# Two 64-row mask matmuls in the row half of their scores, and the values of two heads in one group of 32 columns

## The reference

```python
x = x + attn_a(layernorm(x))   # 16 heads of 8 channels, causal
x = x + ffn(layernorm(x))      # 8 experts, top 2 of each token
x = x + attn_b(layernorm(x))   # 16 heads of 8 channels
x = x + ffn(layernorm(x))

# attn_a
scores = einsum('bhqd,bhkd->bhqk', q, k) / sqrt(8)
attn = softmax(scores + triu(NEG, k=1))
out = einsum('bhqk,bhkd->bhqd', attn, v).transpose(0, 2, 1, 3).reshape(b, t, d)
return out @ wo + bo
```

## Time and profile before

| what | us |
|---|---|
| time, median of 3 runs | 1162.33 |
| lowest, highest | 1160.31, 1164.01 |
| the profiled execution, its span | 1164.9 |
| PE busy | 1029.9 (88%) |
| DVE busy | 755.5 (65%) |
| ACT busy | 672.4 (58%) |
| POOL busy | 525.5 (45%) |
| weight loads of PE | 716.6 (62%) |

### The profile page before, as it was taken

How to read it: one execution, slowest core, us unless ns; L and a number is a source line. 1 busy time by engine, 2 the same in 40 slices (tenths; PEclk the granted TensorE clock), 3 DMA queues, 4 the chain that set the end, 5 groups by cost and what they waited for, 6 DMA issues and landing times.

```text
span 1164.9 us, 28879 instructions
## 1 busy us (share of the span) xinstructions
PE 1029.9 (88%) x9290; PEld 716.6 (62%) x9290; DVE 755.5 (65%) x2322; ACT 672.4 (58%) x1399; POOL 525.5 (45%) x980
## 2 busy tenths in 40 slices
PE   2998999897989999999798979999888799999990
PEld 1444555453468989999443434444443589999990
DVE  4687778877777333456777888888877663334442
ACT  2365676663644545556277858897757445455550
POOL 2243444332742610344687736455736436004455
PEclk9998999996989999999778979998888899999995
DMA  6446544562235878887544323343221469778873
GB/s 152 104 114 138 116 110 99 151 181 57 54 118 174 271 233 236 260 255 236 125 111 104 101 56 85 89 107 84 65 49 44 130 191 280 227 242 256 272 225 109
DMA packets 201723, 175.03 MB, mean 150 GB/s; under 512 B 19812, under 2 KB 160616, under 8 KB 201576
## 3 DMA queue, kind: packets, MB, share of 16 engines
q1 hardware_dynamic: 193384, 156.41, 49.1%
q0 software_dynamic: 8192, 16.79, 4.8%
HBM read 122.99 MB, written 50.14 MB: 149 GB/s over the span
## 4 chain that ended last, share of the span: by engine, by line
PE 60%; DVE 11%; issue 6%; POOL 5%; DMA 4%; SPq 3%; ACT 1%; POOLq 0%; ACTq 0%; DVEq 0%
PE psS L1358 9%; PE psT L1365 9%; PE psO L321 8%; PE psS L355 7%; PE psO L1381 4%; PE psN L1381 4%; DVE mx L671 4%; PE psS L386 3%; PE psT L363 3%; POOL xn L1259 3%; PE psM L276 2%; PE psN L328 2%; DMA eo<-ysb 2%; PE psN L337 1%; PE psM L1346 1%
## 5 line engine op out<-in xcount | busy, mean ns | idle before, releaser
L671 DVE TENSOR_REDUCE mx<-psS 128x3 f32<-128x384 f32 (+1 forms) x512 | 311.4, 617 | 119.5 <-PE psS L386 61.8
L355 PE MATMUL psS<-kst,qst 48*128 48x256 bf16 (+1 forms) x1024 | 201.7, 286 | 46.4 <-DVE mx L671 33.2
L558 ACT ACTIVATE pT<-psT,scb 128x512 f32<-128x512 f32 x256 | 193.9, 777 | 43.2 <-PE psT L363 40.7
L363 PE MATMUL psT<-qst,kst 50*128 50x256 bf16 (+1 forms) x1024 | 194.7, 278 | 4.6 <-DMA qst<-scr_m 2.2
L1422 DVE TENSOR_TENSOR hT<-sg,psT 128x512 f32<-128x512 f32 x142 | 97.5, 686 | 154.4 <-PE psT L1365 127.7
L1245 POOL DMA_INDIRECT xg<-xn,slot x128 | 123.1, 962 | 131.3 <-DVE ysb L1417 72.1
L1358 PE MATMUL psS<-xTt,wgc 128*128 128x128 f32 x1136 | 153.7, 279 | 5.7 <-issue 5.3
L355 PEld LDWEIGHTS psS<-kst,qst 48*128 48x128 bf16 x1024 | 66.2, 97 | 146.0 <-DVE mx L671 68.2
L1365 PE MATMUL psT<-xTt,wuc 128*128 128x128 f32 x1136 | 152.2, 278 | 1.5 <-DMA wuc<-in_L_ffn_Wu 1.4
L790 POOL TENSOR_SCALAR_AFFINE_SELECT pT<-pT 128x256 f32<-128x256 f32 x224 | 90.6, 412 | 133.0 <-ACT pT L553 131.8
L553 ACT ACTIVATE pT<-psT 128x384 f32<-128x384 f32 x256 | 122.9, 490 | 46.1 <-PE psT L363 35.9
(11 more groups left out here) (225 smaller groups left out, 1595.1 us busy)
## 6 DMA issues: line engine op xcount, KB each, us to landing
wgc<-in_L_ffn_Wg SPq DMA_DIRECT2D x142, 256.0 KB, 3.1
wuc<-in_L_ffn_Wu SPq DMA_DIRECT2D x142, 256.0 KB
scr_part<-part SPq DMA_DIRECT2D x128, 128.0 KB, 2.1
qst<-scr_part SPq DMA_DIRECT2D x64, 192.0 KB, 3.7
kst<-scr_part SPq DMA_DIRECT2D x64, 192.0 KB, 4.7
xin<-xg SPq DMA_DIRECT2D x142, 64.0 KB
eo<-ysb SPq DMA_DIRECT2D x142, 64.0 KB
scr_part<-part SPq DMA_DIRECT2D x32, 192.0 KB, 1.9
```

The source lines that it names most:

```text
L355: return nc.tensor.matmul(ps[:, c0:c0 + n], q_[r64, t, q0], k_[r64, t, 0:n], start=(half == 0), stop=True, skip_group_check=True)
L363: return nc.tensor.matmul(ps[:, c0:c0 + T - q0], k_[m64, t, half * P:half * P + P], q_[m64, t, q0:T], start=(half == 0 or not L.causal), s ...
L558: nc.scalar.activation(pT[:, g % 8, 0:cols], psT[g % 2][:, 0:cols], ACT.Exp, scale=scb[r][:, 0, i:i + 1], bias=scb[r][:, 1, i:i + 1]).then ...
L671: nc.vector.tensor_reduce(mx3[:, u, 0:n, pos:pos + 1].rearrange("p a b -> p (a b)"), psS[h % 2][:, 0:kcols(L)].rearrange("p (a k) -> p a k ...
```

## The change

The mask of a head becomes two matmuls of 64 rows each, which lie in the half of the rows that the scores of this head use. The triangles are built anew so that each half of the rows holds a 64-row piece of them; the weights are rows of the identity for the piece on their own half of the partitions, and rows of `identx`, the identity with its column halves exchanged, for the other. The first piece of `trib` covers 128 columns of each diagonal block, the second the last 64. The same is done with `tritb` for the last two batches.

Quads 0 and 2, and quads 1 and 3, now share a group of 32 partitions: the values start at column 16 of a head's 32, and the weights of quads 2 and 3 are read 16 columns further on, so that their values fall on columns 16 to 24 where those of quads 0 and 1 fall on 0 to 8; the four products add up in bank `psO[0]`. So `oT` has two pieces, not four: one copy by ACT at head 2, two transposes at heads 4 and 11. `normalise` picks the heads out of 16-column pieces.

```diff
+HALF_P = P // 2
...
+        identx = sb("identx", [P, P], BF16)
...
-        vp = [sb(f"vp{r}", [P, 2, H, 32]) for r in range(RING)]
+        vp = [sb(f"vp{r}", [P, 2, H * 32 + 16]) for r in range(RING)]
...
-        oT = sb("oT", [P, 4, T])
+        oT = sb("oT", [P, 2, T])
...
-                if q % 2 == 0:
-                    after(pe, s["oT"], 2 * (b - 1) + q // 2 + 1)
+                if q == 0:
+                    after(pe, s["oT"], b)
+                pair, region = q // 2, q % 2
...
-                        o0 = (q % 2) * T
-                        last = nc.tensor.matmul(psO[q // 2][32 * i:32 * i + 32, o0 + dst[0]:o0 + dst[1]],
-                                                vp[r][:, kb, h, :], pT[:, h % 8, src[0]:src[1]],
-                                                start=(kb == 0), stop=(kb == 1), skip_group_check=True)
+                        o0, v0 = region * T, 32 * h + 16 * (1 - pair)
+                        last = nc.tensor.matmul(psO[0][32 * i:32 * i + 32, o0 + dst[0]:o0 + dst[1]],
+                                                vp[r][:, kb, v0:v0 + 32], pT[:, h % 8, src[0]:src[1]],
+                                                start=(q == 0 and kb == 0), stop=(pair == 1 and kb == 1),
+                                                skip_group_check=True)
...
             def out_transposes(qb):
-                for q in range(4):
+                for q in range(2):
...
+            def mask_half(bank, group, half, tri, t0, c0, n):
+
+                rows = slice(HALF_P * group, HALF_P * group + HALF_P)
+                select = identb if half == group else identx
+                diag = bank[:, 0:3 * P].rearrange("p (a k) -> p a k", a=3)[:, 0:3:2, c0:c0 + n]
+                return nc.tensor.matmul(diag, select[rows, :],
+                                        tri[rows, t0:t0 + n].unsqueeze(1).to_broadcast([HALF_P, 2, n]),
+                                        start=False, stop=True, skip_group_check=True)
...
                     if L.causal and bT >= MASKED:
-                        diag = psT[1 - par][:, 0:3 * P].rearrange("p (a k) -> p a k", a=3)[:, 0:3:2, :]
-                        last_t = nc.tensor.matmul(diag, identb[:], tritb[:].unsqueeze(1).to_broadcast([P, 2, P]),
-                                                  start=False, stop=True, skip_group_check=True)
+                        last_t = mask_half(psT[1 - par], 1 - par, 0, tritb, HALF_P, 0, HALF_P)
+                        last_t = mask_half(psT[1 - par], 1 - par, 1, tritb, 0, 0, P)
                     last_t.then_inc(s["ST"], 1)
                 if S_ and L.causal:
-                    last_s = nc.tensor.matmul(psS[par][:, 0:3 * P].rearrange("p (a k) -> p a k", a=3)[:, 0:3:2, :],
-                                              identb[:], trib[:].unsqueeze(1).to_broadcast([P, 2, P]),
-                                              start=False, stop=True, skip_group_check=True)
+                    last_s = mask_half(psS[par], par, 0, trib, 0, 0, P)
+                    last_s = mask_half(psS[par], par, 1, trib, 0, HALF_P, HALF_P)
...
-            def evac_oT(b, half):
-                after(act, s["PV"], 4 * b + 2 * half + 2)
+            def evac_oT(b):
+                after(act, s["PV"], 4 * b + 4)
                 after(act, s["tO_ps"], 2 * b)
-                nc.scalar.activation(oT[:, 2 * half:2 * half + 2, :], psO[half][:].rearrange("p (a t) -> p a t", a=2),
+                nc.scalar.activation(oT[:], psO[0][:].rearrange("p (a t) -> p a t", a=2),
                                      ACT.Copy).then_inc(s["oT"], 1)
...
-                if h == 13 and T_:
-                    evac_oT(bT, 0)
...
-                o4 = psN[:].rearrange("p (h c) -> p h c", c=32)
-                nc.vector.reciprocal(rden[:], o4[:, :, HD]).then_inc(s["rden"], 1)
+                o4 = psN[:, 0:2 * P].rearrange("p (m a c) -> p m a c", a=2, c=2 * HD)
+                den = rden[:].rearrange("p (m a) -> p m a", a=2)
+                nc.vector.reciprocal(den, o4[:, :, :, HD]).then_inc(s["rden"], 1)
...
-            nc.gpsimd.affine_select(out=trib[:], in_=trib[:], compare_op=ALU.is_ge, fill=NEG, base=0,
-                                    pattern=[[-1, P]], channel_multiplier=1).then_inc(s_const, 1)
-            nc.gpsimd.affine_select(out=tritb[:], in_=tritb[:], compare_op=ALU.is_ge, fill=NEG, base=0,
-                                    pattern=[[1, P]], channel_multiplier=-1).then_inc(s_const, 1)
+            for group in range(2):
+                rows = slice(HALF_P * group, HALF_P * group + HALF_P)
+                pool.wait_ge(s_const, 4 + 2 * group)
+                nc.gpsimd.affine_select(out=trib[rows, :], in_=trib[rows, :], compare_op=ALU.is_ge, fill=NEG, base=0,
+                                        pattern=[[-1, P]], channel_multiplier=1).then_inc(s_const, 1)
...
             nc.vector.tensor_copy(identb[:], ident[:]).then_inc(s_const_dve, 1)
+            nc.vector.tensor_copy(identx[:, 0:HALF_P], ident[:, HALF_P:P]).then_inc(s_const_dve, 1)
+            nc.vector.tensor_copy(identx[:, HALF_P:P], ident[:, 0:HALF_P]).then_inc(s_const_dve, 1)
```

More of the change, by code:

```diff
@@ L243, in build, with heads_of @@
         LB.s["pT"] = LB.s["exp"]
+        def heads_of(v):
+            return v[:, :, 0:32 * H].rearrange("p k (h c) -> p k h c", c=32)
         def kcols(L):
@@ L251, in pe_setup @@
             pe.wait_ge(s["wp"], 4)
-            pe.wait_ge(s_const_dve, 2)
+            pe.wait_ge(s_const_dve, 4)
             for o in range(2):
@@ L433, in pe_step @@
                 if h == 4 and O_:
-                    after(pe, s["oT"], 2 * bO + 2)
+                    after(pe, s["oT"], bO + 1)
                     if T_:
@@ L534, in act_step @@
                 if h == 2 and O_:
-                    evac_oT(bO, 1)
+                    evac_oT(bO)
                 if h == (3 if L.causal else 4) and P_:
@@ L639, in normalise @@
                 after(dve, s["onT_ps"], 2 * bO + qb)
-                o4 = psN[:].rearrange("p (h c) -> p h c", c=32)
-                nc.vector.reciprocal(rden[:], o4[:, :, HD]).then_inc(s["rden"], 1)
+                o4 = psN[:, 0:2 * P].rearrange("p (m a c) -> p m a c", a=2, c=2 * HD)
+                den = rden[:].rearrange("p (m a) -> p m a", a=2)
+                nc.vector.reciprocal(den, o4[:, :, :, HD]).then_inc(s["rden"], 1)
                 after(dve, s["rden"], 2 * bO + qb + 1)
-                nc.vector.tensor_tensor(out=on[:].rearrange("p (h c) -> p h c", c=HD), in0=o4[:, :, 0:HD],
-                                        in1=rden[:].unsqueeze(2).to_broadcast([P, H, HD]),
+                nc.vector.tensor_tensor(out=on[:].rearrange("p (a m c) -> p m a c", a=2, c=HD), in0=o4[:, :, :, 0:HD],
+                                        in1=den.unsqueeze(3).to_broadcast([P, 8, 2, HD]),
                                         op=ALU.mult).then_inc(s["on"], 1)
@@ L705, in dve_step @@
                         ins = nc.vector.tensor_tensor(
-                            out=vp[rS][:, k, :, 0:HD], in0=psM[:, k * P:(k + 1) * P].rearrange("p (h c) -> p h c", c=HD),
+                            out=heads_of(vp[rS])[:, k, :, 16:16 + HD], in0=psM[:, k * P:(k + 1) * P].rearrange("p (h c) -> p h c", c=HD),
                             in1=L.b_wide[:, 0, :].rearrange("p (h c) -> p h c", c=HD), op=ALU.add)
@@ L775, in pool_step @@
                     for r in range(RING):
-                        nc.gpsimd.memset(vp[r][:, :, :, HD:HD + 1], 1.0).then_inc(s_mset, 1)
+                        nc.gpsimd.memset(heads_of(vp[r])[:, :, :, 16 + HD:17 + HD], 1.0).then_inc(s_mset, 1)
             if not L.causal and 0 <= j - 1 < B:
@@ L991, in pe_route @@
             if k == ROUTE_T:
-                pe.wait_ge((LA, LB)[l].s["oT"], 2 * B)
+                pe.wait_ge((LA, LB)[l].s["oT"], B)
                 pe_tokens(pe, n, QUADS[1] - 1)
@@ L1570, in hook @@
                     if h == 6:
-                        pe.wait_ge(L.s["oT"], 2 * (j - 4) + 2)
                         for i in range(2):
@@ L1605, in hook @@
                     if h == 3:
-                        pe.wait_ge(L.s["oT"], 2 * B - 1)
+                        pe.wait_ge(L.s["oT"], B)
                     pe_logits(pe, n + 1, h // 3 - 1)
@@ L1755, in _ @@
                                     pattern=[[-1, P]], channel_multiplier=1).then_inc(s_const, 1)
-            nc.gpsimd.affine_select(out=trib[:], in_=trib[:], compare_op=ALU.is_ge, fill=NEG, base=0,
-                                    pattern=[[-1, P]], channel_multiplier=1).then_inc(s_const, 1)
-            nc.gpsimd.affine_select(out=tritb[:], in_=tritb[:], compare_op=ALU.is_ge, fill=NEG, base=0,
-                                    pattern=[[1, P]], channel_multiplier=-1).then_inc(s_const, 1)
+            for group in range(2):
[3 more added lines that the diff above has]
+                                        pattern=[[-1, P]], channel_multiplier=1).then_inc(s_const, 1)
```

(9 more changed lines are left out.)

1 line of the change is left out of this document (removed).

## The result

The changed kernel takes 1178.82 us (median of 4 runs, 1173.81 to 1183.49) against 1162.66 us before (median of 4, 1160.31 to 1164.01): a ratio of 1.014, 95% interval 1.0107 to 1.0173. It is 16 us slower, where 5 us faster was forecast. The profiled execution took 1180.46 us. That of the kernel before, 1164.9 us long by its span alone, is slower than its timed runs, so the spans differ by 13.6 us where the medians differ by 16.2.

A forecast was written before the change was run, and what follows sets the result against it. A steady step was taken to be bound by a chain of PE and DVE pieces. Layer A -3.1, layer B -2.1 and start +0.3 gave -4.9 us: 1160.0 for the profiled execution, 1157.4 us as median; range 1150 to 1165.

The forecast's parts named there:

- The chain of a steady step: Layer A's steady step, 15.88 us: a chain of PE and DVE pieces; only shortening a piece on it counts.
- A: The causal attention layer: a steady step was to get 0.22 us shorter, between 0.13 and 0.3.
- (c): Rival at the masks: the gap before them stays and they grow, 14 x 0.25 = +3.5 us, 1165.4 or 1164; chance 0.12.
- The packing: Both layers: four of eight output transposes a step go, 0.22 us of PE at head 4 and again at head 11.
- PE's before head 1: PE's idle before head 1 in a steady step of layer A, forecast to grow past 0.45 us.
- (a): Rival, PE alone the bound: every saved PE piece counts, 0.95 us a step in A, 19 us in all, 1143; chance 0.08.
- B: The attention layer without mask: gains at heads 5 and 15, 0.15 us a step, 14 x 0.15 = 2.1 us.
- The start: Kernel start: DVE makes `identx` in two half-size casts on the path to the first transposes, at most +0.3 us.
- no change: Whole kernel: times within 0.3%, 3.5 us, counted as not told apart, from 1158.8 to 1165.8; based on three runs' spread.
- 14 x 0.22: Layer A, batches 2 to 15: each of 14 steps saves 0.22 us, 3.1 us in all.
- (d): Rival: PE idling more where DVE paces lowers the clock, 6.0 us per such step, two give 1169; chance 0.08.
- the sign named for (d): Trace of layer A: a lower granted clock between 115 and 210 us would show (d).

The follow-up runs named there:

- e1: Kernel before with only the new 64-row masks; values, copies and transposes as before: 1181.15 us, 16.9 over before.
- e2: Changed kernel with the old single 128-row mask matmul, so the packing alone: 1163.59 us, 0.7 under before.
- e8: Changed kernel with each causal mask as two matmuls over all 128 rows, 64 columns of both blocks each: 1171.29 us, 6.6 over before.
- e9: e6 with old 128-row masks from head 13 of step 5 to the end of step 6, and of 13 to 14: 1168.80 us, 5.5 over before.
- e12: Kernel before with 64-row masks only from head 13 of step 5 to the end of step 6, and of 13 to 14: 1171.69 us.
- e6: Changed kernel with SP's extra load of steps 5 and 13 issued behind the row maxima, not ahead: 1176.43 us, 11.7 over before.
- e3: Changed kernel with each output transpose made twice, eight a step as before: 1175.34 us, 11.1 over before.
- e7: Kernel before with more of SP's extra loads issued ahead of the row maxima in steps 5 and 13: 1177.33 us, 12.6 over before.
- e10: e8 with SP's extra load of steps 5 and 13 behind the row maxima, as in e6: 1168.78 us, 5.5 over before.
- e5: Kernel before with the unread matmuls of e4 at the same places: 1164.64 us, 0.1 under before.
- e13: e2 with the unread matmuls of e4 at the same places: 1163.18 us, 0.6 under before.
- e4: Changed kernel with unread matmuls where PE stands before heads 8 and 13 of steps 5 and 13, layer A: 1164.96 us, 0.7 over before.

## Why the prediction was wrong

*The chain of a steady step* was right, and a little too careful in A. The mask starts at 0.17 and not at 0.27, so (c) did not happen; six undisturbed steps give 1.95/6 = 0.33 each, not 0.22. The packing brings most of it: the masks alone (e1) take 95.5 us for these steps, no less than the 95.3 before, the packing alone (e2) 94.0; the links through DVE's maxima do swallow what the masks save. DVE's and PE's waits sit where they were put, PE's before head 1 longer by 0.12. (a) did not happen: PE gives 0.95 a step by its own pieces and a third of it arrives. In B 0.10, not 0.15. The start cost 0.5, not 0.3, in one execution each. (The three runs behind "no change" lay within 0.17% of their median, not 0.16%; nothing hangs on it.)

*The packing* was put at a small gain; alone it is 1163.59, no change that can be told.

*The step that failed* is the sum's "14 x 0.22", together with the place that (d) gave to the clock. The sum priced 14 steps of A by a timeline at the full clock. Six of them are like that (7 to 12), and there the clock stayed at 1.00, so the sign named for (d), a lower clock between 115 and 210 us, never showed. But steps 5, 6, 13 and 14 had half clock before the change already, and the row that showed such a stretch (0.50 in the earlier trace rows) was used only to price a rival of chance 0.08. In these four the change costs 9.7 us in the profiled execution, not -0.9.

*The mechanism of (d)* was half right. It looked for PE idling more where DVE paces. Shown is something else: where PE's standing has brought the half clock, it stays longer with 64-row masks (e8, e9, e12), and the second mask instruction brings late row maxima and one more standing (e6, e8). In steps 5 and 6 every execution with 64-row masks behind the standing and no filler has 14 to 20 us at half clock (after, e1, e3, e6, e12), every one with 128-row masks 7 to 10 (before, e2, e7, e8, e9, e10); in steps 13 and 14 the two groups overlap. By medians, each against its own kernel before, full rows in place of half rows take 16.2 to 6.6 us (e8), early maxima 16.2 to 11.7 (e6, intervals overlap), both 16.2 to 5.5 (e10).

*Open.* Where the 5.5 us of e10 lie, and as much in the changed kernel: of the 13.6 between the two profiled executions, 5.8 stand outside the four steps and the six in the middle, none over 2.4 in one stretch, and one execution of each kernel doesn't tell such a sum from scatter. Whether shorter steps 5, 6, 13 and 14 (e5, e13) shorten the whole. And how a transfer of instructions comes to hold SP's issues.

## What to carry to other kernels

A saving read off an undisturbed step counts only for the steps that are like it: list the stretches at the lower clock first and price the change there by itself. Making a matmul narrower in rows can cost more than it saves where PE has just stood and must win its clock back; here full-row masks in the stretch behind the standing took 4.5 us less over four steps (e6 to e9). Where PE must wait anyway, matmuls that nobody reads can keep its clock up: here they brought the time from 16.2 to 0.7 us over the kernel before. And an edit that adds instructions to one engine can delay another's transfers, so compare their timelines too.

## What the hardware showed beyond that

The granted clock does not follow the busy share that the profile shows. At 4.00 of 4 us busy it stayed at 0.50 in e6, and at 3.83 of 4 it was 0.93 in e9, where the masks had twice the rows. The Trainium skill, TensorE: Matmul & The Clock Gate, What's actually happening, says that a monitor of PE's activity sets the clock; what the profile counts as busy does not tell it in these rows.

A second instruction for each mask, on PE, moves SP's issues: the maxima of step 5 were issued 4.6 to 4.8 us after its first scores in the kernels with whole masks up to there (before, e2, e5, e12, e13) and 5.7 to 6.0 us after in those with two pieces (after, e1, e3, e4, e8). SP issues the same 1122 transfers in each of them. What moves is a transfer on the queue `q8 instruction` (16 KB each, 77 in the kernel after): in the first group it comes 6.6 to 7.0 us after those scores, in the second 2.5 to 3.1, just where the held issue is. This holds in general here: from 30 to 300 us of all 15 executions, 58 of SP's 3843 issues took over 1.5 us, and 57 of these overlap such a transfer, while 425 of all issues do. So the transfer goes with the hold, but does not bring it each time.
